# A two-block transformer kernel: the cross attention context of block 0 is prepared two ticks earlier, and its last copy moves within VectorE's tick

## The reference, cut to what matters

```
h = ln(x)*(1+sc1) + sh1;  x += attn(h@Wq.., h@Wk.., h@Wv..) @ Wos       # self attention, 16 heads of 16
h = ln(x)*(1+sc2) + sh2;  x += attn(h@Wq, context@Wk, context@Wv) @ Woc # cross attention, context is [128, 192] per sequence
h = ln(x)*(1+sc3) + sh3;  x += gelu(h@W1 + b1) @ W2
```

## Time and profile before

| | |
|---|---|
| median of 3 runs | 4402.54 us (4395.08 to 4405.3) |
| the profiled execution, its own time | 4394.15 us |
| its span | 4392.0 us |
| granted clock over the span | 0.987 |
| busy: PE, DVE, ACT, POOL | 94%, 67%, 63%, 63% |

### The profile page before, as it was taken

One profiled execution on the slowest core, in us unless ns is written; L12 is line 12 of the kernel. 1 busy time (PEld: TensorE's weight loads), 2 busy tenths in 40 slices (PEclk: granted clock), 3 DMA queues, 4 the chain that ended last, 5 costly groups with the idle time before them and its releaser, 6 DMA issues.

```text
span 4392.0 us, 95934 instructions
## 1 busy us (share of the span) xinstructions
PE 4145.6 (94%) x34934; PEld 3514.9 (80%) x34934; DVE 2959.7 (67%) x6250; ACT 2745.7 (63%) x10788; POOL 2758.7 (63%) x2555
## 2 busy tenths in 40 slices
PE   7999989888889999999999999999999999999999
PEld 5777777777779987888888888778787878787998
DVE  7999988889865556555556565666666666665443
ACT  5999888888863335656565666656565656564332
POOL 4666666666667775555555565666666666665776
PEclk9999999999999999999999999999999999999999
DMA  2110011111111122222222222322222222221110
GB/s 74 33 33 30 31 41 37 45 45 36 44 55 49 40 73 80 73 75 73 73 75 73 73 78 86 101 75 85 74 86 74 86 73 86 74 91 61 49 46 33
DMA packets 229269, 276.65 MB, mean 63 GB/s; under 512 B 37948, under 2 KB 160320, under 8 KB 228800
## 3 DMA queue, kind: packets, MB, share of 16 engines
q1 hardware_dynamic: 228732, 270.51, 18.0%
q10 hardware_dynamic: 68, 0.02, 0.0%
HBM read 85.89 MB, written 50.33 MB: 31 GB/s over the span
## 4 chain that ended last, share of the span: by engine, by line
PE 65%; DVE 20%; ACT 8%; issue 5%; POOL 2%; DMA 0%; ACTq 0%; SPq 0%; POOLq 0%; DVEq 0%
PE BANKS L573 15%; PE BANKS L575 14%; PE BANKS L574 14%; PE BANKS L724 6%; PE BANKS L712 6%; PE BANKS L760 5%; DVE NM L995 4%; DVE PT L1002 3%; ACT PR L880 2%; ACT PR L864 2%; DVE WL L1044 1%; DVE Z L1101 1%; ACT HF L908 1%; DVE ST L1091 1%; PE BANKS L769 1%
## 5 line engine op out<-in xcount | busy, mean ns | idle before, releaser
L1180 POOL TENSOR_TENSOR PR<-PR,RL 128x512 f32<-128x512 f32 x1024 | 1069.5, 1045 | 946.0 <-DVE RL L1007 942.5
L880 ACT ACTIVATE PR<-BANKS,NM 128x128 f32<-128x128 f32 x2048 | 730.0, 384 | 487.8 <-DVE NM L1058 431.0
L864 ACT ACTIVATE PR<-BANKS,NM 128x128 f32<-128x128 f32 x2048 | 728.9, 415 | 3.9 <-DVE NM L995 3.8
L573 PE MATMUL BANKS<-HH,WH 128*128 128x512 f32 x1632 | 691.7, 424 | 38.0 <-DVE SN L1072 26.7
L1058 DVE TENSOR_REDUCE NM<-BANKS 128x8 f32<-128x1024 f32 x256 | 312.7, 1222 | 532.2 <-PE BANKS L724 532.1
L760 PE MATMUL BANKS<-ID,PR 128*128 128x128 f32 x4096 | 632.9, 278 | 40.6 <-DVE OL L1051 22.8
L575 PE MATMUL BANKS<-HH,WL 128*128 128x512 f32 x1632 | 644.5, 395 | 0.0
L574 PE MATMUL BANKS<-HL,WH 128*128 128x512 f32 x1632 | 644.2, 395 | 0.0
L760 PEld LDWEIGHTS BANKS<-ID,PR 128*128 128x128 f32 x4096 | 496.0, 142 | 165.1 <-issue 61.9
L864 ACT ACTIVATION_READ_ACCUMULATOR PR<-BANKS,NM 128x1 f32 x2048 | 520.1, 257 | 0.0
L1203 POOL TENSOR_TENSOR GL<-GF,GH 128x512 fp32r<-128x512 f32 x256 | 342.4, 1338 | 206.1 <-DVE GH L1147 206.1
(11 more groups left out here) (123 smaller groups left out, 10825.9 us busy)
## 6 DMA issues: line engine op xcount, KB each, us to landing
SW<-SN SPq DMA_DIRECT2D x1024, 128.0 KB, 2.0
x_scratch<-X SPq DMA_DIRECT2D x80, 512.0 KB, 3.2
X<-x_scratch SPq DMA_DIRECT2D x80, 512.0 KB, 4.0
CX<-in_ctx SPq DMA_DIRECT2D x32, 384.0 KB, 4.2
X<-in_x SPq DMA_DIRECT2D x16, 512.0 KB, 3.8
out<-X SPq DMA_DIRECT2D x16, 512.0 KB, 2.9
CX<-in_ctx SPq DMA_DIRECT2D x32, 128.0 KB, 3.8
STG<-in_L_xcond_W SPq DMA_DIRECT2D x4, 512.0 KB, 5.0
```

The costliest lines, as they stand in the source:

```text
L573: e.matmul(o, lh, rh, start=first and i == 0, stop=False)
L864: made = e.activation(pr[:, r], bank[:, r], ACT.Exp, bias=nm[:, h:h + 1], accum_out=RL[npr(t)[0]][:, h:h + 1])
L880: made = e.activation(pr[:, r], bank[:, r], ACT.Exp, bias=nm[:, h:h + 1], accum_out=RL[npr(t)[0]][:, h:h + 1])
L1180: e.tensor_tensor(p3, p3, RL[npr(t)[0]][:, :].unsqueeze(2).broadcast_to([128, 4, 128]), ALU.mult).then_inc(s_nrm, 1)
```

## The change

Of stage 1 only: the context's load, its transposes, its copy from PSUM and its split come two ticks earlier. The transposes move to slots 0 and 1, the copy to 1 and 2, the split to 2 and 3; the merge stays at slot 6. Of stages 1 and 4: within DVE's tick, the merge goes from behind the reciprocal to behind `c_split`, which is behind all of that tick's attention and layer norm steps.

```diff
             if p in CROSS:
-                at["load_c", tg - (22 if p == 1 else 16)].append((p, g))
+                at["load_c", tg - (24 if p == 1 else 16)].append((p, g))
...
                 for c in range(2):
-                    at["c_turn", tg - (14 if p == 1 else 8) + c].append(Part(p, g, c, 0))
-                    at["c_hf", tg - (13 if p == 1 else 8) + c].append(Part(p, g, c, 0))
-                    at["c_split", tg - (12 if p == 1 else 7) + c].append(Part(p, g, c, 0))
+                    at["c_turn", tg - (16 if p == 1 else 8) + c].append(Part(p, g, c, 0))
+                    at["c_hf", tg - (15 if p == 1 else 8) + c].append(Part(p, g, c, 0))
+                    at["c_split", tg - (14 if p == 1 else 7) + c].append(Part(p, g, c, 0))
                 at["c_merge", tg - (10 if p == 1 else 5)].append((p, g))
...
                     e.reciprocal(rl[:, :], rl[:, :]).then_inc(s_rl, 1)
 
-                for p, g in at["c_merge", tick]:
-                    u, k = h_of(p, g, True)
-                    q.wait_ge(s_hl, 2 * u + 2)
-                    e.tensor_copy(HH[k][64:128, 1, :], HL[k][64:128, 1, :].bitcast(F)).then_inc(s_hm, 1)
-
                 for x in at["v_out", tick]:
...
                     e.tensor_copy(HH[k][:, x.c, :], HF[u % 2][:, x.c, :]).then_inc(s_hh, 1)
 
+                for p, g in at["c_merge", tick]:
+                    u, k = h_of(p, g, True)
+                    q.wait_ge(s_hl, 2 * u + 2)
+                    e.tensor_copy(HH[k][64:128, 1, :], HL[k][64:128, 1, :].bitcast(F)).then_inc(s_hm, 1)
+
                 for p, g, j in at["up", tick]:
```

## The result

The changed kernel takes 4441.1 us (median of 4 runs, 4438.4 to 4448.2), the kernel before 4400.0 us beside it. The ratio is 1.0096 with a 95% interval of 1.0078 to 1.0114: slower by about 41 us. The direction was forecast, the size was not: 4414 was forecast, with 4430 as the end of the range.

A forecast was written before the change was run, and what follows sets the result against it. It took DVE and PE as both near full in stage 1, the chain of waits changing between them. 15 x 1.1 = 16.5, -1.5 (last group), -3 (clock) gave +12 us: 4406 profiled, 4414 on the median, range 4380 to 4430.

The forecast's parts named there:

- `p_turn` of slot 1 behind OL: PE, slot 1: newly dealt bank makes `p_turn` wait for OL's read-out; DVE's copy of it starts 0.34 us late.
- RS starts behind HL and Z waits: POOL, slot 2: `c_split` stands ahead of `root`, so RS ends at 1042.84 and DVE stands 0.9 us at Z.
- the upper of the two cases: Slots 3 and 6: DVE gets in behind POOL's instruction; copy ends at 1044.9, not 1044.0, merge at 1052.4, not 1051.75.
- Stage 4: Merge behind QT and SN still ends about 3253.5, with 1.8 us of cover before `k1`; 0 us at both ends.
- the clock term: Stage 1, PE's lower clock after the stall ahead of `k`: stall 2.68 to about 2.3 us, taken as -3 us.
- its bound: Clock at worst: a 0.50 stretch in every period, 1.7 us each, 25.5 in place of 17.5 us, +8.
- idle time of slots 5 and 6: PE is held 1.5 us at slot 5 and 0.3 us at slot 6 behind OL.
- Rival 2: Clock: PE idle spread over slots 5 to 7 lowers the clock every period; +24.5 us, 4427; chance 0.07.
- one meeting with GpSimd: Slot 4: Z waits for POOL's second HL, ends at 1046.4 to 1046.5; the step behind it is 2.3 us late.
- the rule that I had used for the merge: Slot 6: POOL has asked first while DVE is still writing, so +1.1 us a period, nearer the upper end.
- the last group: Stage 1's last context, no layer norm beside it: loses the 0.70 us wait and some of 1.25; -1.5 us once.
- Rival 3: Faster: RS ends before 1041.9, so Z does not wait; 24 us less plus clock, 4361 to 4378; chance 0.20.

The follow-up runs named there:

- c: The changed kernel with RS put ahead of `c_split` in GpSimd's tick, in stage 1 only; 4405.9 us, ratio 1.0010 to before.
- d: The changed kernel with RS ahead of `c_split` in GpSimd's tick and the merge back behind the reciprocal; 4375.6 us, ratio 0.9945 to before.
- a: The kernel before with only the merge moved behind `c_split`, the context at its old ticks; 4384.1 us, ratio 0.9962 to before.
- i: The changed kernel with the context one tick earlier than before in place of two, the merge last in the tick; ratio 1.0015 to before.
- b: The changed kernel with the merge back behind the reciprocal, so only the two ticks earlier remain; ratio 1.0015 to before.
- filled kernels: Several kernels, before and changed among them, with slot 6's transposes repeated as idle PE work; before so filled has ratio 0.9949, changed so filled 1.0022.
- g: The changed kernel with the merge right behind V, ahead of Z, in VectorE's tick; ratio 1.0047 to before.

## Why the prediction was right in direction and wrong in size

**Right, as worked out.** `p_turn` of slot 1 behind OL makes DVE's copy 0.34 us late, as forecast (13.05 us behind WL of slot 12, 12.7 before). RS starts behind HL and Z waits 0.85 us, 15 times (0.9). The copy of slot 3 and the merge come behind the product and the bias, the upper of the two cases. `k` waits 2.4 us for the merge at the end (2.3). Stage 4 is unchanged. That RS could not pass HL is what c and d show: let it pass, and 1.4 us a period are gone. The Trainium skill's rule of first in, first out (TensorE: Matmul & The Clock Gate, Architectural detail) spoke against this change, and the trace agrees: RS starts at 1125.08, behind HL of 1123.82, in the period above.

**Wrong: the clock term.** It was taken as -3 us with +8 as its bound; it is +17.6 (18.4 to 36.0). The step that failed is "I take -3, since the one long stall is somewhat shorter", and with it the bound, a stretch like that of the earlier trace rows in each period. The stall is shorter, 2.4 us in place of 2.7, and the idle time of slots 5 and 6 was seen too (1.5 and 0.3 forecast, 1.0 and 1.1 measured); but the second was given no price. With both there is no period without a fall, and in 10 of 15 the lower clock costs 2.9 to 3.0 us, where the most before was 2.1. Rival 2 had the mechanism, with too small a price. Two rows of one such period, whose `k` starts at about 1050.7; the clock is at 0.50 through all the windows between them:

```profile
1050.00:1051.00 1.00, 0.33 (x1) 0.50 0.00 0
...
1059.00:1060.00 1.00, 1.00 (x7) 0.50 1.07 294
```

These ten microseconds cost 15.62 - 12.65 = 2.97 us. The longest stretches before were of seven and cost 1.7 to 2.1. A bound taken from the stretches of the old kernel does not hold for a new pattern of idle.

**Wrong: one meeting with GpSimd.** A period was forecast 1.1 us longer (0.55 to 1.2) and is 2.04 longer. The step that failed is that of slot 4: "Z waits for POOL's second HL in either case and ends at 1046.4 to 1046.5". Z was issued at 1129.37, POOL's HL ended at 1129.47, but the product had its turn first (1129.43), and Z ended 0.14 us behind that, at 1130.62. What follows this Z is 3.2 us later than before, not 2.3 (counted from WL of slot 12), and slots 5 and 6 then take what was forecast. These 0.9 us are nearly all that is missing. Written with the rule that I had used for the merge (POOL first where it has asked first), the sum would have been 1.1 + 0.85, and 15 x 1.95 is 29 us in place of 16.5.

**Wrong: the last group**, -1.5 forecast, -2.4 measured (25.37 to 22.93): it loses the wait and the long merge (0.42 us now); what else is in it stays open.

With 15 x 2.04 = +30.6 for the periods (the first context and the 14 of the table), -2.4 and +17.6 the forecast's own sum would be +46. With the 5.1 us ahead of the stage and the 2.1 less behind it that is the 48.9 of the profiled executions; the medians differ by 41.

**A reading that nothing shows:** VE stands in the prediction among the steps that stretch beside POOL. It takes 0.85 us in every period of both kernels, and in stage 0 too, so no row shows it stretched; no term of the sum rests on it.

**What it did not see** is that the two parts work against each other: each was priced inside the other's setting, so that a faster version (a, 16 us) lay in the change unseen. Rival 3 (faster) named one right point, RS before Z asks for it. But that alone does not give its 4361 to 4378: with RS in time and the merge last (c and i) the kernel takes 4406, a little more than before. Only with the merge first as well (d and j) does it come to 4375.6 and 4375.9, and that is no longer the change as made.

## What to carry to other kernels

When a step is moved to an earlier tick, look at what it now stands ahead of in each engine's queue, on the least loaded engine too: a 1.3 us step ahead of a 1 us one that feeds the critical engine cost 1.4 us a period here, and one exchange of their order gave it back. Price two parts of a change separately before together; a copy put last in a tick is free while its input is late and is dear once its input is early. And where TensorE stands still for one to three microseconds in each period, price its clock with a run, not from the stretches that the old kernel shows.

## What the runs showed of the hardware

- The granted clock fell to 0.50 in all 15 periods with a stall of 2.4 to 2.5 us ahead of `k` and waits of 0.5 us or more at slots 5 and 6 (changed, c, i); in 11 and 7 of 15 with 2.7 and 2.2 us and no such waits (before, a); in 12 and 5 of 15 with 1.3 us (b, d); and in none or one with the 0.4 to 0.9 us left in the filled kernels. What a period lost by it lay near 1.3, between 1.6 and 2.2, or near 3.0 us, for work that is the same each time.
- Idle repeats of a transpose, 1.7 us a period, made the kernel before faster by 23 us (f), with everything else as it was.
- A DVE copy or Z from SBUF that met a POOL instruction ended about 0.14 us (Z) or 0.3 us (copy) behind it in the rows shown here: the same 64x512 copy took 0.42 us (b), 0.83 (changed), 1.00 (g), 1.15 (a) or 1.25 us (before) by what POOL was doing. The Trainium skill (SBUF — State Buffer, Who interferes with whom) says that whoever issues first has the shared pair of ports for the whole instruction and that the other is blocked, not slowed. The trace agrees, 1.25 against 0.42 us, and adds that DVE can come behind two POOL instructions in a row: in slot 4 its Z started 0.10 us before HL ended and yet came behind the product that followed. That it lost because it asked so late is a reading of these rows; no run tests it.
